# Cross-attention with two score spans: probabilities turned by VectorE in 32x32 blocks and carried across partitions by DMAs, main loop interleaved by feature tile

## The chip, the cores and the metric

The kernel runs on one core of a Trainium2 chip. The metric is the time of the whole program on the device in microseconds (us). A core has TensorE (matmuls), VectorE, ScalarE and GpSimd (element by element work), and SyncE, which here only issues DMAs; the engines run side by side and meet at semaphores. TensorE reads SBUF and writes PSUM, eight banks of 128 partitions x 512 fp32 values.

## The reference

`x` is 8 x 1024 x 640, the context 8 x 64 x 1024. The first 56 tokens are text, the last 8 are 4 dummy and 4 image tokens, whose scores get a mask. There are 20 heads of 32 features.

```python
q = _split_heads(hidden_states @ w_q, HEADS)
k = _split_heads(text @ w_k, HEADS)
v = _split_heads(text @ w_v, HEADS)
out_text = _merge_heads(_sdpa(q, k, v))
mask_ip = _ip_mask(bbox, B, S, hidden_states.dtype)
k_ip = _split_heads(ip_h @ w_k_ip, HEADS)
v_ip = _split_heads(ip_h @ w_v_ip, HEADS)
out_ip = _merge_heads(_sdpa(q, k_ip, v_ip, mask=mask_ip))
out = (out_text + IP_SCALE * out_ip) @ w_out + b_out + residual
```

`_sdpa` is softmax(q k / sqrt(32) + mask) v, one softmax over the text keys and another over the 8 image and dummy keys.

## The kernel before

Queries are worked on in 16 groups of 512 (two for each of the 8 batches). All is laid out with features first: `xT`, `qT` and the output have the feature in the partition, five tiles of 128 features (four heads each). For full precision every large product is made of parts: an operand is rounded to `hi` by ScalarE, `lo` is the rest (by VectorE or GpSimd), and `three` adds hi x hi, hi x lo and lo x hi (L97 to L99).

A setup of about 97 us makes keys and values of all batches, and the queries, scores and softmax of group 0. Then each group g is done in two stages on TensorE:

- `scores(g)`: 80 score matmuls (L203) in eight units of PSUM, the output product of group g-1 (`out_tile`, 75 matmuls of 512 columns), and the first two of the five query tiles of group g+1 (`q_steps`). Beside it ScalarE copies scores to `prob` (L209), GpSimd adds the mask and subtracts the maxima (L238, L169), VectorE finds maxima and sums (L224, L230), ScalarE takes exponentials (L216) and GpSimd multiplies by the inverse sums (L175). All this goes by tiles of 128 queries, `tile(t)`, 20 heads x 64 keys wide.
- `values(g)`: a pair p of heads (2 x 64 keys = 128 rows) needs its probabilities with the key in the partition. `transpose_tile` (L1189) turns four 128 x 128 squares of `prob` on TensorE into a PSUM bank, ScalarE rounds the bank to `pT_hi` (L695), VectorE subtracts to get `pT_lo` (L940). `pv_pair` multiplies both by the pair's values (L1204, L1205), ScalarE moves half of the result (L700), VectorE adds the halves to `o_raw` (L947), ScalarE and GpSimd split that into `oT_hi` (L704) and `oT_lo` (L533). Between pairs TensorE does the last three query tiles of group g+1.

VectorE also makes `xT_lo` (L111, both inputs in SBUF) and adds the residual to the output (L957); ScalarE makes the residual `res` (L710). SyncE loads `xin` (L466) and stores the output (L473). Each engine runs its own list in the order written; nothing is reordered.

## Time and profile before

| | us |
|---|---|
| median of three runs | 849.45 (849.35 to 849.67) |
| the profiled execution | 849.42 |
| its span, first to last instruction | 847.6 |
| busy TensorE | 840.3 (99%) |
| busy VectorE | 625.6 (74%) |
| busy ScalarE | 581.8 (69%) |
| busy GpSimd | 507.2 (60%) |

The busy time of an engine is what it worked within the span; TensorE's matmuls are pipelined, so its busy share tells that it is fed, not that each matmul runs at its peak. The granted TensorE clock is at its higher level (2.4 GHz) in every slice of the page. DMA engines are busy 22% of their time.

### The profile page before, as it was taken

How to read it: one execution, taken by the hardware profiler on the slowest of the kernel's cores; microseconds unless marked ns; L12 is line 12 of the kernel's file. 1: busy time of each engine (PE TensorE's matmuls, PEld its weight loads, DVE VectorE, ACT ScalarE, POOL GpSimd, SP SyncE). 2: the span in 40 equal slices, each digit the busy share in tenths (PEclk: the TensorE clock that was granted, in tenths of full speed). 3: DMA queues.
4: the chain of work that ended last, by engine and by line, in shares of the span. 5: the costliest groups of instructions: out<-in, count | busy, mean ns of one | idle time of the engine just before them, and what ended most of it. 6: DMA issues, size and time to landing. Idle time of an engine off the chain costs nothing.

```text
span 847.6 us, 13817 instructions
## 1 busy us (share of the span) xinstructions
PE 840.3 (99%) x5036; PEld 708.4 (84%) x5036; DVE 625.6 (74%) x923; ACT 581.8 (69%) x987; POOL 507.2 (60%) x405
## 2 busy tenths in 40 slices
PE   9999999999999999999999999999999999999998
PEld 8889888888888888888888888888888888888877
DVE  6839877695867768695867769586766869587785
ACT  7756676866767585776768586775768577674773
POOL 0059778293756749294755839385664929375581
PEclk9999999999999999999999999999999999999999
DMA  9934223012030402104030401204030310310012
GB/s 316 387 98 133 93 79 132 1 35 107 1 132 1 140 1 90 43 2 139 1 132 1 140 2 39 94 1 140 2 131 2 101 39 2 123 38 26 2 49 75
DMA packets 34295, 65.06 MB, mean 77 GB/s; under 512 B 4544, under 2 KB 6848, under 8 KB 34112
## 3 DMA queue, kind: packets, MB, share of 16 engines
q1 hardware_dynamic: 33952, 62.84, 21.6%
q10 hardware_dynamic: 288, 1.44, 0.4%
q8 instruction: 40, 0.66, 0.3%
q14 instruction: 15, 0.12, 0.0%
HBM read 40.34 MB, written 23.59 MB: 75 GB/s over the span
## 4 chain that ended last, share of the span: by engine, by line
PE 80%; POOL 14%; ACT 3%; issue 2%; DVE 0%; DMA 0%; ACTq 0%; SPq 0%; POOLq 0%; DVEq 0%
PE bank L97 18%; PE bank L99 18%; PE bank L98 18%; PE bank L1189 8%; POOL prob L169 7%; PE bank L203 6%; POOL prob L175 6%; PE bank L1204 4%; PE bank L1205 4%; ACT prob L209 2%; PE bank L1087 1%; PE bank L1095 1%; POOL wo_lo L498 1%; PE bank L1099 1%; POOL prob L238 1%
## 5 line engine op out<-in xcount | busy, mean ns | idle before, releaser
L533 POOL TENSOR_TENSOR oT_lo<-o_raw,oT_hi 128x512 fp32r<-128x512 f32 x63 | 81.4, 1293 | 208.1 <-ACT oT_hi L704 208.0
L947 DVE TENSOR_TENSOR o_raw<-bank,pv_part 64x512 f32<-64x512 f32 x160 | 110.2, 689 | 100.3 <-ACT pv_part L700 97.8
L169 POOL TENSOR_TENSOR prob<-prob,top 128x1120 f32<-128x1120 f32 x126 | 180.1, 1458 | 0.7 <-DVE top L224 0.7
L175 POOL TENSOR_TENSOR prob<-prob,inv 128x1120 f32<-128x1120 f32 x126 | 178.3, 1449 | 0.0
L97 PE MATMUL bank<-xT_hi,wq_hi 128*128 128x512 f32 x400 | 162.8, 407 | 0.0
L97 PE MATMUL bank<-oT_hi,wo_hi 128*128 128x512 f32 (+1 forms) x405 | 159.2, 393 | 2.0 <-ACT res L756 2.0
L98 PE MATMUL bank<-oT_lo,wo_hi 128*128 128x512 f32 (+1 forms) x405 | 156.7, 387 | 0.0
L99 PE MATMUL bank<-oT_hi,wo_lo 128*128 128x512 f32 (+1 forms) x405 | 156.7, 387 | 0.0
L99 PE MATMUL bank<-xT_hi,wq_lo 128*128 128x512 f32 x400 | 156.6, 391 | 0.0
L98 PE MATMUL bank<-xT_lo,wq_hi 128*128 128x512 f32 x400 | 155.9, 390 | 0.0
L940 DVE TENSOR_TENSOR pT_lo<-bank,pT_hi 128x512 fp32r<-128x512 f32 x158 | 102.0, 686 | 56.1 <-ACT pT_hi L695 54.1
L216 ACT ACTIVATE prob<-prob 128x1280 f32<-128x1280 f32 x64 | 81.7, 1277 | 78.2 <-POOL prob L169 78.2
L700 ACT ACTIVATE pv_part<-bank 64x512 f32<-64x512 f32 x160 | 94.8, 592 | 58.3 <-PE bank L1205 55.8
L224 DVE TENSOR_REDUCE top<-prob 128x20 f32<-128x1120 f32 (+1 forms) x128 | 98.2, 812 | 31.0 <-ACT prob L209 20.9
L125 ACT ACTIVATE qT<-bank 128x512 f32<-128x512 f32 x80 | 47.7, 596 | 86.6 <-PE bank L99 86.6
L230 DVE TENSOR_REDUCE total<-prob 128x20 f32<-128x1120 f32 (+1 forms) x128 | 97.9, 805 | 1.7 <-ACT prob L216 1.7
L97 PEld LDWEIGHTS bank<-oT_hi,wo_hi 128*128 128x128 f32 x405 | 76.1, 188 | 20.0 <-ACT res L756 2.4
L695 ACT ACTIVATE pT_hi<-bank 128x512 fp32r<-128x512 f32 x158 | 86.1, 596 | 8.0 <-PE bank L1189 6.4
L99 PEld LDWEIGHTS bank<-oT_hi,wo_lo 128*128 128x128 f32 x405 | 76.1, 188 | 15.7
L99 PEld LDWEIGHTS bank<-xT_hi,wq_lo 128*128 128x128 f32 x400 | 75.1, 188 | 16.4
L98 PEld LDWEIGHTS bank<-oT_lo,wo_hi 128*128 128x128 f32 x405 | 76.1, 188 | 14.7
L98 PEld LDWEIGHTS bank<-xT_lo,wq_hi 128*128 128x128 f32 x400 | 75.4, 189 | 13.3
(118 smaller groups left out, 1352.8 us busy)
## 6 DMA issues: line engine op xcount, KB each, us to landing
outT<-res SPq DMA_DIRECT2D x79, 256.0 KB, 6.7
xin<-in_xT SPq DMA_DIRECT2D x15, 1280.0 KB, 6.8
w_raw<-in_L_xattn_w_k SPq DMA_DIRECT2D x8, 320.0 KB, 5.4
w_raw<-in_L_xattn_w_k_ip SPq DMA_DIRECT2D x8, 320.0 KB, 5.7
w_raw<-in_L_xattn_w_v_ip SPq DMA_DIRECT2D x8, 320.0 KB, 4.3
w_raw<-in_L_xattn_w_v SPq DMA_DIRECT2D x8, 320.0 KB, 3.2
v_raw<-v_scratch SPq DMA_DIRECT2D x14, 140.0 KB
prob<-in_textT SPq DMA_DIRECT2D x8, 224.0 KB, 4.6
```

The lines of the kernel that those rows point to most:

```text
L97: nc.tensor.matmul(dst, a_hi, b_hi, start=first, stop=False)
L98: nc.tensor.matmul(dst, a_hi, b_lo, start=False, stop=False)
L99: return nc.tensor.matmul(dst, a_lo, b_hi, start=False, stop=last)
L169: ins = eng.tensor_tensor(s, s, top[:, t, n, :].unsqueeze(2).broadcast_to([P, HEADS, k1 - k0]), ALU.subtract)
L175: ins = eng.tensor_tensor(s, s, inv[:, t, n, :].unsqueeze(2).broadcast_to([P, HEADS, k1 - k0]), ALU.mult)
L216: nc.scalar.activation(prob[:, t * SW:(t + 1) * SW], prob[:, t * SW:(t + 1) * SW], ACT.Exp).then_inc(exp_done, 1)
L224: ins = nc.vector.tensor_reduce(top[:, t, n, :], tile(t)[:, :, k0:k1], AX.X, ALU.max)
L230: nc.vector.tensor_reduce(total[:, t, span, :], tile(t)[:, :, k0:k1], AX.X, ALU.add).then_inc(sum_done, 1)
L695: nc.scalar.activation(pT_pair(g, p)[0], pT_bank(g, p)[:], ACT.Copy).then_inc(pT_hi_done, 1)
L700: nc.scalar.activation(pv_part[own, :], v_bank[p % 2][other, :], ACT.Copy).then_inc(pv_moved, 1)
L940: nc.vector.tensor_tensor(lo, pT_bank(g, p)[:], hi.bitcast(F32), ALU.subtract).then_inc(pT_lo_done, 1)
L947: nc.vector.tensor_tensor(o_raw[own, m % 2, :], v_bank[p % 2][own, :], pv_part[own, :], ALU.add).then_inc(pv_added, 1)
```

## The change

The probabilities are no longer turned by TensorE. In place of four query tiles the softmax now goes by five chunks m, one for each feature tile: `chunk(m)` holds 4 heads x 4 tiles x 64 keys = 1024 columns. When a chunk is normalised, VectorE turns its 32x32 blocks in place of partition quarters (`turn`, one instruction for 1024 columns) into `stage`, and SyncE carries the blocks to the right quarter of the partitions, back into `prob` (`hand_over`: 16 DMAs of 32 partitions for each of three shares of a group: chunks 0 and 1, 2 and 3, 4). ScalarE rounds from there to `pT_hi`; `pT_lo` is made by VectorE for even pairs and by GpSimd for odd ones, both from SBUF. The columns of a pair come in another order, which `add_pv` undoes as it writes.

The main loop of TensorE is one list for each group g: pairs 0 and 1, scores of chunk 0 of g+1, output tiles 3 and 4 of g-1, the last step of its tiles 0 to 2, and then four times two pairs, one chunk of scores of g+1, three output steps of g and one query tile of g+2. The other engines' lists follow that. The residual is loaded from HBM (`load_res`) instead of copied by ScalarE, and the bias is added with it. `oT_lo` is all made by GpSimd. The special last group is gone, and so are the loops with a counter: each list is written out in full. `stage` has four slots; chunk 4 shares the slot of chunk 3.

```diff
+        def chunk(m):
+            return prob[:, m * CHUNK:(m + 1) * CHUNK].rearrange("p (r k) -> p r k", k=KEYS)
...
+            m, r = divmod(n, 2)
+            return prob[:, m * CHUNK:(m + 1) * CHUNK].rearrange("p (t r c) -> p r t c", r=2, c=PW)[:, r]
...
+        def turn(dve, g, m):
+
+            before = (g, 3) if m == 4 else (g - 1, 4) if m == 3 else (g - 1, m)
+            dve.wait_ge(prob_done, KD * g + m + 1)
+            if before[0] >= 0:
+                landed(dve, *before)
+            src = prob[:, m * CHUNK:(m + 1) * CHUNK].rearrange("p (t c i) -> p t c i", t=GT, i=QUAD)
+            dst = stage[:, stage_slot(m)].rearrange("p c (t i) -> p t c i", i=QUAD)
+            nc.vector.transpose(dst, src).then_inc(turned, 1)
...
+                def hand_over(g, share):
+                    m0, m1 = SHARES[share]
+                    turns = stage[:].rearrange("p s (h c) t -> p (s h) c t", c=QUADS)
+                    pairs = prob[:].rearrange("p (n q t) -> p n q t", q=QUADS, t=P)
+                    s0 = 2 * stage_slot(m0)
+                    sp.wait_ge(turned, KD * g + m1)
+                    for q in range(QUADS):
+                        for c in range(QUADS):
+                            sp.dma_start(pairs[c * QUAD:(c + 1) * QUAD, 2 * m0:2 * m1, q, :],
+                                         turns[q * QUAD:(q + 1) * QUAD, s0:s0 + 2 * (m1 - m0), c, :]).then_inc(pT_landed[share], 16)
...
+                    hand_over(g, 2)
+                    if g > 0:
+                        for m in OUT_ORDER:
+                            store(g - 1, m)
...
+                    if g + 1 < NG:
+                        hand_over(g + 1, 0)
+                    if g + 3 < NG:
+                        load_x(g + 3)
+                    load_res(g)
+                    if g + 1 < NG:
+                        hand_over(g + 1, 1)
...
+                    pool.wait_ge(pT_hi_done, PAIRS * g + p + 1)
+                    nc.gpsimd.tensor_tensor(pT_at(pT_lo, g, p), pT(p), pT_at(pT_hi, g, p).bitcast(F32), ALU.subtract).then_inc(pT_lo_pool, 1)
...
-                    act.wait_ge(pT_ready, PAIRS * g + p + 1)
-                    nc.scalar.activation(pT_pair(g, p)[0], pT_bank(g, p)[:], ACT.Copy).then_inc(pT_hi_done, 1)
+                    landed(act, g, p // 2)
+                    wait(act, pv_ready, PAIRS * g + p + 1 - P_RING)
+                    nc.scalar.activation(pT_at(pT_hi, g, p), pT(p), ACT.Copy).then_inc(pT_hi_done, 1)
...
+                    if more:
+                        pT_part(n, 0)
+                        pT_part(n, 1)
+                        pT_part(n, 2)
+                    if more_x:
+                        move_q(act, x, 3)
+                    if more:
+                        pT_part(n, 3)
...
+                    if more_x:
+                        x_lo_part(dve, x, 0)
                     add_pv(g, 0)
                     add_pv(g, 1)
-                    pT_part(g, 3)
-                    oT_part(g, 0)
+                    if more_x:
+                        x_lo_part(dve, x, 1)
+                        x_lo_part(dve, x, 2)
+                    if g > 0:
+                        output(g - 1, 3)
+                    if more_x:
+                        x_lo_part(dve, x, 3)
+                    if g > 0:
+                        sums(dve, g, 4)
+                        output(g - 1, 4)
+                        output(g - 1, 0)
+                    if more:
+                        maxima(dve, n, 0)
+                    if g > 0:
+                        output(g - 1, 1)
+                        output(g - 1, 2)
+                    if more_x:
+                        x_lo_part(dve, x, 4)
+
                     add_pv(g, 2)
                     pT_part(g, 4)
                     add_pv(g, 3)
-                    pT_part(g, 5)
-                    for p in range(4, PAIRS):
-                        add_pv(g, p)
-                        for n in last_transposes_of(p):
-                            pT_part(g, n)
-                    oT_part(g, KD - 1)
-
-                def values(g, build=False):
-                    pT_part(g, 0)
-                    pT_part(g, 1)
-                    if build:
-
-                        dve.wait_ge(v_stored, 48)
-                    for s in range(KD):
-                        for p in (2 * s, 2 * s + 1):
-                            add_pv(g, p)
-                        if s < KD - 1:
-                            for p in (2 * s + 2, 2 * s + 3):
-                                pT_part(g, p)
-
-                def group(g, u):
-                    softmax(g, u)
-                    values(g)
-
-                dve.wait_ge(v_zeroed, 1)
-                v_lo_part(dve, 0)
-                values(0, True)
-                softmax(1, 1)
-                values(1)
-                for b in range(1, B - 1):
-                    group(2 * b, 0)
-                    group(2 * b + 1, 1)
-                softmax(NG - 2, 0)
-                values(NG - 2)
-                last_softmax(NG - 1)
-                last_values(NG - 1)
-                for m in range(KD - 1):
-                    output(NG - 1, 1, m, last_banks)
-                for n, (bk, q) in enumerate(last_halves):
-                    dve.wait_ge(out_ready, KD * NG + n)
-                    r = res[:, 1, KD - 1, q]
-                    nc.vector.tensor_tensor(r, bk[:, 0:q.stop - q.start], r, ALU.add).then_inc(out_done, 1)
+                    turn(dve, g, 4)
+                    if more:
+                        maxima(dve, n, 1)
+                        sums(dve, n, 0)
+
+                    add_pv(g, 4)
+                    add_pv(g, 5)
+                    pT_part(g, 6)
+                    if more:
+                        sums(dve, n, 1)
+                        maxima(dve, n, 2)
+                        turn(dve, n, 0)
+                        turn(dve, n, 1)
+
+                    add_pv(g, 6)
+                    add_pv(g, 7)
+                    pT_part(g, 8)
+                    if more:
+                        maxima(dve, n, 3)
+                        sums(dve, n, 2)
+
+                    add_pv(g, 8)
+                    add_pv(g, 9)
+                    if more and n % GPB == 0:
+                        v_lo_part(dve, n // GPB)
+                    if more:
+                        sums(dve, n, 3)
+                        turn(dve, n, 2)
+                        maxima(dve, n, 4)
+                        pT_part(n, 0)
+                        pT_part(n, 2)
+                        turn(dve, n, 3)
...
-                def transpose_tile(g, p, t):
-                    src = prob[:, t * SW + p * P:t * SW + (p + 1) * P]
-                    return nc.tensor.transpose(pT_bank(g, p)[:, t * P:(t + 1) * P], src, ident[:])
...
+                for g in range(NG):
+                    pv_pair(g, 0)
+                    pv_pair(g, 1)
+                    if g + 1 < NG:
+                        next_scores(g + 1, 0)
+                    if g > 0:
+                        long_outs(g - 1)
+                        for m in range(3):
+                            out_step(g - 1, m, KD - 1)
...
+                        pv_pair(g, 2 * s)
+                        pv_pair(g, 2 * s + 1)
+                        if g + 1 < NG:
+                            next_scores(g + 1, s)
+                        wide_outs(g, s - 1)
+                        if g + 2 < NG:
+                            if s == 1:
+                                wait(pe, out_done, outs_before(g - 1, 3) + 1)
+                            pe.wait_ge(q_moved, KD * (g + 1) + KD - 1 if s == 1 else KD * (g + 2) + s - 1)
+                            q_steps(pe, g + 2, s - 1)
+                    if g + 2 < NG:
+                        pe.wait_ge(score_copied, UNITS * (g + 1) + 2 * KD - 1)
+                        q_steps(pe, g + 2, KD - 1)
+                wide_outs(NG - 1, KD - 1)
```

What stands in a row on TensorE between the pairs, before (in the stage of values; L1189 is the turning, L97 to L99 one step of a query tile):

```order
L1204 MATMUL bank<-pT_hi,v_parts 128x512
L1205 MATMUL bank<-pT_lo,v_parts 128x512
L1189 MATMUL bank<-ident,prob 128x128 x8
L97 MATMUL bank<-xT_hi,wq_hi 128x512
L98 MATMUL bank<-xT_lo,wq_hi 128x512
L99 MATMUL bank<-xT_hi,wq_lo 128x512
```

and now (L196 are the scores of one chunk, L100 to L102 one output step):

```order
L1166 MATMUL bank<-pT_hi,v_parts 128x512
L1167 MATMUL bank<-pT_lo,v_parts 128x512
L196 MATMUL bank<-k_diag,qT 128x128 x8
L100 MATMUL bank<-oT_hi,wo_hi 128x512
L101 MATMUL bank<-oT_lo,wo_hi 128x512
L102 MATMUL bank<-oT_hi,wo_lo 128x512
```

The turning is gone from between the pairs, and the scores, which stood in one block before the output product, have moved there in five pieces.

VectorE around the border of two groups, before (end of the softmax of a group, then its pairs):

```order
L957 TENSOR_TENSOR res<-bank,res 128x512
L230 TENSOR_REDUCE total<-prob 128x20 x2
L232 RECIPROCAL inv<-total 128x40
L940 TENSOR_TENSOR pT_lo<-bank,pT_hi 128x512 x2
L947 TENSOR_TENSOR o_raw<-bank,pv_part 64x512 x2
```

and now (L237 is `turn`, of chunk 2 and then of chunk 3; the next group begins at the first L117):

```order
L237 STREAM_TRANSPOSE stage<-prob 128x4x8x32
L216 TENSOR_REDUCE top<-prob 128x16 x2
L946 TENSOR_TENSOR pT_lo<-prob,pT_hi 128x512 x2
L237 STREAM_TRANSPOSE stage<-prob 128x4x8x32
L117 TENSOR_TENSOR xT_lo<-xin,xT_hi 128x512
L956 TENSOR_TENSOR o_raw<-bank,pv_part 64x4x4x32 x2
L117 TENSOR_TENSOR xT_lo<-xin,xT_hi 128x512 x2
L962 SCALAR_TENSOR_TENSOR res<-bank,bias,res 128x512
```

The turning of chunk 3 stands last in a group's list, behind two `pT_lo` of the next group, and all five `xT_lo` and five outputs stand at the head of the list, ahead of the second pair.

SyncE in one group, now (before there were one load and five stores, and in some groups the small ones of keys and values):

```order
L462 DMA prob<-stage 32x4x128 x16
L467 DMA xin<-in_xT 128x5x512
L471 DMA res<-in_xT 128x5x512
L462 DMA prob<-stage 32x4x128 x16
L462 DMA prob<-stage 32x2x128 x16
L497 DMA outT<-res 128x512 x5
```

These are `hand_over` of shares 0, 1 and 2 (L462), 48 DMAs for each group, with the two loads and the stores in the same list.

## Rows read from the trace of the kernel before

**Rows 1.** the page's first part: busy time of each engine over the span

```profile
PE 840.3 (99%) x5036; PEld 708.4 (84%) x5036; DVE 625.6 (74%) x923; ACT 581.8 (69%) x987; POOL 507.2 (60%) x405
```

**Rows 2.** busy us of each engine in five stretches of one group each (x is a count)

```profile
164.04:212.55 48.51, 48.46 (x291) 40.37 (x290) 36.40 (x53) 33.42 (x57) 30.37 (x24) 1.00 0.18 62
...
sum 241.50, PE 241.41 PEld 201.82 DVE 179.07 ACT 169.79 POOL 151.60; mean PE 48.28 PEld 40.36 DVE 35.81 ACT 33.96 POOL 30.32
```

**Rows 3.** TensorE by the chain of work that ended last, 305 to 320 us: start, us, what

```profile
305.38 0.88 PE bank L1189 x8
...
309.24 4.83 PE bank L203 x80
314.07 0.43 PE bank L97
314.50 0.23 PE bank L98
```

**Rows 4.** groups of instructions by line and shape: operands, shapes, count | busy us, mean ns | idle before

```profile
L947 DVE TENSOR_TENSOR o_raw<-bank,pv_part 64x512 f32<-64x512 f32 x160 | 110.2, 689 | 100.3 <-ACT pv_part L700 97.8
L940 DVE TENSOR_TENSOR pT_lo<-bank,pT_hi 128x512 fp32r<-128x512 f32 x158 | 102.0, 686 | 56.1 <-ACT pT_hi L695 54.1
...
L1189 PE MATMUL bank<-ident,prob 128*128 128x128 f32 x640 | 84.7, 273 | 0.3
L111 DVE TENSOR_TENSOR xT_lo<-xin,xT_hi 128x512 fp32r<-128x512 f32 x80 | 84.3, 1068 | 0.0
L224 DVE TENSOR_REDUCE top<-prob 128x20 f32<-128x1120 f32 x64 | 84.0, 1312 | 20.9 <-ACT prob L209 20.9
...
L533 POOL TENSOR_TENSOR oT_lo<-o_raw,oT_hi 128x512 fp32r<-128x512 f32 x63 | 81.4, 1293 | 208.1 <-ACT oT_hi L704 208.0
...
L704 ACT ACTIVATE oT_hi<-o_raw 128x512 fp32r<-128x512 f32 x80 | 51.0, 637 | 3.0 <-DVE o_raw L947 2.6
...
L175 DVE TENSOR_TENSOR prob<-prob,inv 128x1120 f32<-128x1120 f32 x1 | 2.4, 2417 | 0.0
```

**Rows 5.** one line's instructions, L111 and then L940: count, duration ns min/median/max

```profile
L111 DVE TENSOR_TENSOR xT_lo<-xin,xT_hi x80: 626/682/2551, 26.6 to 765.5; 128x512 fp32r<-128x512 f32 x80
L940 DVE TENSOR_TENSOR pT_lo<-bank,pT_hi x158: 673/686/693, 98.1 to 833.5; 128x512 fp32r<-128x512 f32 x158
```

**Rows 6.** VectorE in order of time: start us, us, line, operation, idle before

```profile
327.38 0.63 DVE L111 TENSOR_TENSOR xT_lo<-xin,xT_hi 128x512 fp32r<-128x512 f32 x1
...
330.43 2.51 DVE L111 TENSOR_TENSOR xT_lo<-xin,xT_hi 128x512 fp32r<-128x512 f32 x1
...
339.54 1.29 DVE L940 TENSOR_TENSOR pT_lo<-bank,pT_hi 128x512 fp32r<-128x512 f32 x2 [4.11 <-ACT pT_hi L695]
```

**Rows 7.** GpSimd in order of time, the same columns

```profile
327.29 10.88 POOL L175 TENSOR_TENSOR prob<-prob,inv 128x1120 f32<-128x1120 f32 x8
344.61 1.29 POOL L533 TENSOR_TENSOR oT_lo<-o_raw,oT_hi 128x512 fp32r<-128x512 f32 x1 [6.45 <-ACT oT_hi L704]
```

**Rows 8.** SyncE issuing DMAs, 3 to 5 us and later: start us, us, line, out<-in

```profile
3.06 0.43 SPq L413 DMA_DIRECT2D prob<-in_ipT  x1
3.53 0.43 SPq L407 DMA_DIRECT2D w_raw<-in_L_xattn_w_k_ip  x1
...
89.45 0.95 SPq L440 DMA_DIRECT2D v_raw<-v_text  x1
...
91.96 0.65 SPq L441 DMA_DIRECT2D v_raw<-v_ip  x1
...
235.92 2.74 SPq L473 DMA_DIRECT2D outT<-res  x5
```

**Rows 9.** the page's DMA issues: operands, queue, count, KB each, us to landing

```profile
xin<-in_xT SPq DMA_DIRECT2D x15, 1280.0 KB, 6.8
...
outT<-res SPq DMA_DIRECT2D x1, 128.0 KB, 1.8
```

**Rows 10.** the page's DMA queues: packets, MB, share of 16 engines

```profile
q1 hardware_dynamic: 33952, 62.84, 21.6%
```

More of the change, by code:

```diff
@@ L200, in score_units, with score_unit @@
+        def score_unit(pe, g, m):
+            pe.wait_ge(q_moved, KD * g + m + 1)
+            for t in range(GT):
                 q_cols = slice(t * P, (t + 1) * P)
@@ L575, in group @@
-                def group(g):
-                    softmax(g)
-                    values(g)
-                values(0, True)
-                group(1)
-                with pool.Fori(1, B - 1) as b:
-                    group(2 * b)
-                    group(2 * b + 1)
-                group(NG - 2)
-                last_softmax(NG - 1)
-                for m in range(KD):
-                    add_x(m)
-                for m in range(1, KD - 1):
-                    oT_part(NG - 1, m)
+                    nc.gpsimd.tensor_tensor(oT_at(oT_lo, g, m), o_raw[:, (KD * g + m) % 2, :], oT_at(oT_hi, g, m).bitcast(F32), ALU.subtract).then_inc(oT_lo_done, 1)
@@ L805, in group @@
-                def group(g, u, b):
-                    softmax(g, u, b)
-                    values(g)
                 v_hi_part(0)
@@ L898, in _ @@
                     lo_chunk(c)
-                for t in range(GT):
-                    maxima(dve, 0, t)
+                for m in range(KD):
+                    maxima(dve, 0, m)
                 lo_chunk(behind[0])
@@ L1022, in last_values @@
+                dve.wait_ge(v_zeroed, 1)
+                v_lo_part(dve, 0)
+                turn(dve, 0, 2)
+                turn(dve, 0, 3)
+                pT_part(0, 0)
+                pT_part(0, 2)
+                dve.wait_ge(v_stored, 48)
+                for g in range(NG):
+                    n, x = g + 1, g + 2
+                    more, more_x = n < NG, x < NG
+                    if more_x:
+                        x_lo_part(dve, x, 0)
                     add_pv(g, 0)
                     add_pv(g, 1)
-                    pT_part(g, 3)
@@ new lines, in _ @@
+                    add_pv(g, 8)
+                    add_pv(g, 9)
+                    if more and n % GPB == 0:
+                        v_lo_part(dve, n // GPB)
+                    if more:
+                        sums(dve, n, 3)
[4 more added lines that the diff above has]
+                        turn(dve, n, 3)
+                for m in OUT_ORDER:
+                    output(NG - 1, m)
@@ L1171, in _ @@
                         ins.then_inc(k_ipT_ready, 1)
[L1172 to L1173 removed]
+                for m in range(KD):
+                    if m == 0:
+                        pe.wait_ge(k_built, HPT)
+                    elif m >= 3:
+                        pe.wait_ge(score_copied, 2 * m - 4)
+                    score_unit(pe, 0, m)
                 for k in range(KC):
@@ new lines, in _, with pv_pair @@
+                pe.wait_ge(q_moved, KD + 2)
+                q_steps(pe, 1, 4)
+                pe.wait_ge(w_lo_done[0], len(dve_chunks))
+                def pv_pair(g, p):
+                    n = PAIRS * g + p
+                    if p == 0 and g % GPB == 0:
+                        pe.wait_ge(v_built, 2 * (g // GPB + 1))
+                    wait(pe, pv_added, n - 1)
+                    pe.wait_ge(pT_lo_pool if p % 2 else pT_lo_dve, KD * g + p // 2 + 1)
+                    v = v_parts[:, p, :, :].rearrange("p s c -> p (s c)")
+                    nc.tensor.matmul(v_bank[p % 2][:], v, pT_at(pT_hi, g, p), start=True, stop=False)
+                    nc.tensor.matmul(v_bank[p % 2][:], v, pT_at(pT_lo, g, p), start=False, stop=True).then_inc(pv_ready, 1)
@@ L1319, in group, with next_scores @@
[L1319 to L1330 removed]
+                def next_scores(g, m):
+                    if m == 0:
+                        pe.wait_ge(q_moved, KD * (g + 1))
+                        pe.wait_ge(score_copied, UNITS * g)
+                        if g % GPB == 0:
+                            pe.wait_ge(k_built, HPT * (g // GPB + 1))
+                    else:
+                        if m == 1 and g > 1:
+                            pe.wait_ge(out_done, outs_before(g - 2, 4) + 1)
+                        pe.wait_ge(score_copied, UNITS * g + 2 * m)
+                    score_unit(pe, g, m)
@@ new lines, in wide_outs, with long_outs @@
+                def wide_outs(g, k):
+                    for m in (3, 4, 0, 1, 2) if g == NG - 1 else range(3):
+                        if k == 0 and g > 0:
+                            pe.wait_ge(out_done, outs_before(g - 1, m) + 1)
+                        out_step(g, m, k)
+                def long_outs(g):
+                    pe.wait_ge(q_moved, KD * min(g + 3, NG) - (1 if g + 2 < NG else 0))
+                    for k in range(KD):
+                        out_step(g, 3, k)
+                    pe.wait_ge(score_copied, min(UNITS * (g + 2) + 1, UNITS * NG))
+                    for k in range(KD):
+                        out_step(g, 4, k)
```

776 lines of the change are left out of this document (288 added, 488 removed).

## The prediction

> **What bounds the kernel now.** I read the page's first part, then the busy time in single groups, then the chain that ended last, then the groups of instructions, and last the issue of DMAs. TensorE is busy 840.3 of the span's 847.6 us [rows 1]; a group takes 48.3 us on average and TensorE has no gap in it, while VectorE is busy 35.8, ScalarE 34.0 and GpSimd 30.3 us [rows 2]. So the period of a group is TensorE's own work, and what leaves TensorE's list leaves the time, until another engine's list is as long. In the chain the eight transposes between two pairs take 0.88 us, so 0.11 us each [rows 3]. 80 score matmuls take 4.83 us; the matmul of 512 columns behind them takes 0.43 in place of 0.23 us, so the step from scores to a full matmul costs 0.20 us [rows 3].
>
> **TensorE's part of the change.** It loses 640 transposes [rows 4], 640 x 0.11 = 70.4 us, or 4.4 us a group. The 170 matmuls of 512 columns of a group and its 80 score matmuls stay. The scores now stand in five places instead of one, so four more steps of 0.20 us in each of 15 groups: 60 x 0.20 = 12 us (between 0, if the step were hidden, and 12). TensorE's list for a group is then 48.3 - 4.4 + 0.8 = 44.7 us. Both ends of the program change: at the start query tiles 2 to 4 of group 1 no longer lie between pairs, at the end the hand-made last group is gone, and the last chunk is turned, carried, rounded, multiplied, added and split with only output steps beside it. I estimate 5 us for both (bounds 0 and 12: the carrying alone is some 9 us, of which output steps hide most). Against the profiled execution's 849.4 (span 847.6 and 1.8 around it; the median is 849.45, the same): 849.4 - 70.4 + 12 + 5 = **796 us** if TensorE never waits.
>
> **What the others get, for each group.** VectorE, from 35.8 us [rows 2]:
> - ten `pT_lo` from PSUM leave, 1.29 us for two [rows 6]: -6.5.
> - five `pT_lo` with both inputs in SBUF come. The same shape is `xT_lo`: 0.63 us when alone and 2.51 us when it starts while GpSimd is in a subtraction or multiplication [rows 5, 6, 7]; its mean is 1.07 [rows 4], about 1.0 from start to start. So +5.0, bounds 3.2 and 12.6.
> - five `turn` of 1024 columns come, an operation the trace doesn't have. The lower bound is a pass at the pace of the reduction (1312 ns for 1120 columns [rows 4]), 1.2 us; the upper is the pace of VectorE's slowest row, 2417 ns for 1120 [rows 4], 2.2 us. I take 1.2, since it has one input and one pass: +6.0, bounds 6.0 and 11.
> - one more chunk to reduce and invert +0.7, one `oT_lo` less -0.6 (estimates from the same rows).
>
> Sum 40.4 us, bounds 38.6 and 53. GpSimd: 30.3 + 1.3 for the fifth `oT_lo` + 5 x 1.29 = 6.5 for `pT_lo` [rows 4] + 1 for five smaller pieces instead of four + 1.6 of waiting for VectorE's two-input instructions (0 to 3.2) = 40.7 us. ScalarE loses the residual and stays near 31. So beside 44.7 us of TensorE stand 40.4 and 40.7: the cover falls from 12 and 18 us to 4.
>
> The Trainium skill, SBUF — State Buffer, "Who interferes with whom", says that a VectorE instruction with two SBUF inputs contends with a GpSimd instruction that reads SBUF, and that the second to issue waits for the whole of the first; `L940`, with PSUM as one input, never leaves 673 to 693 ns [rows 5], so the trace agrees. This speaks against the change, which moves five instructions from the free kind to the other and makes GpSimd busy nearly always. Vector Engine (DVE) Microarchitecture Reference, section 3.8, says that the 32x32 transpose sustains one element per cycle per lane; at its clock that would be 1.07 us for 1024, near my lower bound; no row here shows it.
>
> **The carrying.** 48 DMAs a group, all on SyncE. An issue costs 0.47 us from start to start at the program's start and 2.74/5 = 0.55 for stores, but 2.51/3 = 0.84 for the only three gaps between copies from SBUF to SBUF [rows 8]. I take 0.5, as those three also had few and odd partitions, 56 and 8. One share is 16 x 0.5 = 8 us and lands 2 us later (1.8 for the smallest [rows 9]). The data: 5 x 1024 columns x 128 partitions x 4 bytes = 2.6 MB, 5120 packets of 512 bytes a group, 320 for each DMA engine. At the mean time of a packet now (21.6% of 16 x 847.6 us over 33952 packets = 86 ns [rows 10]) that is 28 us, at its mean rate by bytes 8 us; the old traffic adds 11. So it fits in 44.7 us, and one share moves as fast as it is issued or 3 us slower.
>
> **Where it closes.** In steady state these form a ring through three lists: VectorE's `turn` of chunk 4 -> SyncE's share 2 (16 issues), five stores 2.7, now and then keys and values 1.2 -> share 0 of the next group (16 issues), landing 2 -> ScalarE's three `pT_hi` 1.9 [rows 4] -> VectorE's `pT_lo` 1.0 and `turn` of chunk 3 1.2 -> the head of VectorE's next list (five `xT_lo`, two additions, five outputs, sums of chunk 4, maxima of chunk 0: 5.0 + 1.4 + 3.4 + 1.9 + 1.3 = 13.0, durations by rows 4) -> an addition, `pT_lo`, an addition, `turn` of chunk 4 (3.6). Together 26.6 us + 32 issues. At 0.5 that is 42.6, under TensorE's 44.7; it reaches 44.7 at 0.57 and the present 48.3 at 0.68 us. The other place with little room is that head: TensorE asks for the third output bank 14.4 us into the group, and the 13.0 us of VectorE's head end at about 13.5. GpSimd can't begin a list before ScalarE's first `oT_hi`, some 8 us in, so its 40.7 us reach 4 us into the next group. Each delay there is one of TensorE's. I put 0.9 us of waiting on each of 15 groups, between 0 and 2: 13.5 us. **796 + 14 = 810 us**.
>
> **Rivals.**
> 1. *No waiting to speak of.* The slack of 4 us is enough; 796 to 800. For it: the ring at 0.47 is 41.6 us. Against it: three lists at over 90% of the period with fixed orders.
> 2. *VectorE and GpSimd become the bound through the shared port.* If the ten two-input instructions wait 1.6 us on average in place of 1.0 and GpSimd loses as much, VectorE is at 44 to 46 and with the waits of its ring a group takes some 47.3: 796 + 15 x 2.6 = 835 (822 to 848). For it: 2.51 [rows 6] and GpSimd's share going from 63% to 91%. Against: the mean of 80 `xT_lo`, most of which fell into GpSimd's busiest time, is 1.07.
> 3. *Slower: SyncE's issue sets the ring.* One mechanism, from 0.68 us an issue on. At 0.75 a group takes 26.6 + 24 = 50.6 and the time is 796 + 15 x 5.9 = 885; at 0.84 it is 925. For it: 0.84 for copies within SBUF [rows 8], and DMA engines at 86 ns a packet would take 8 x 86 = 0.69 for each issue and hold it back. Against it: every other row is at 0.43 to 0.55, whatever the number of pieces.
> 4. *Slower: `turn` takes two passes,* 2.2 us. VectorE is at 45.4 before it waits for anything, and the ring has two of them; a group takes 49 to 50: 796 + 15 x 4.7 = 866. For it only that VectorE's 4-byte transpose is in no row.
>
> That the change doesn't do what it says is no rival: no transpose stands between the pairs in the new list.
>
> **How the numbers follow.** Forecast, 801 to 821: 0.42. Rival 1: 0.13. Rival 2: 0.24. Rival 3: 0.13. Rival 4: 0.08. The predicted time is 810 us. Leaving out rivals 3 and 4 from 860 up is nearly 0.2, so the range goes from 796 to 855, which holds rivals 1 and 2 and the edge of 3 (0.69 us an issue gives 859). Within 0.2% of 849.4, about what a measurement of this kernel can tell from no change, is 0.03, taken from rivals 2 and 3; faster 0.77, slower 0.20.
>
> **What would show it.** No L1189 group, and full matmuls still 0.23 us apart: the 70 us. The first matmul behind each chunk of scores at 0.43: the 12 us. The `turn` group's mean at 1.2 or at 2.2 us: rivals 1 and 4 apart. `pT_lo` from SBUF at a mean of 1.0 or over 1.6, and GpSimd's waits: rival 2. Starts of the 48 issues 0.5 or over 0.68 us apart, and ScalarE waiting for the carried blocks: rival 3. Stretches from one group's scores to the next: 44.7 is rival 1, 45.6 the forecast, over 48.3 slower. The forecast is wrong at its root if TensorE's busy time doesn't fall by some 60 us, or if its waits are for something in none of the lists above.

## The result and the profile after

The changed kernel takes **875.5 us** (median of 4 runs, 873.9 to 879.7) beside 849.4 for the kernel before (849.35 to 849.67): ratio 1.030, 95% interval 1.028 to 1.033. It is slower by 26 us; forecast were 810 us and a range from 796 to 855. The profiled execution is the 873.9 one, with a span of 872.1 us.

The first part of its page, then the chain that ended last, by engine and by line (the lines that answer to [rows 1]):

```profile
span 872.1 us, 13091 instructions
...
PE 814.0 (93%) x4381; PEld 650.9 (75%) x4381; DVE 670.6 (77%) x983; ACT 541.3 (62%) x928; POOL 624.1 (72%) x576
...
PEclk9999989999999999899999999999999999999898
...
SPq 45%; DVE 17%; PE 15%; DMA 11%; issue 7%; ACT 4%; POOL 1%; ACTq 0%; DVEq 0%
```

TensorE lost only 26 us of busy time, where 58 were forecast, and now idles 58 us, where it idled 7. The chain runs through SyncE's queue for 45% of the span. The carrying DMAs are `L462`; its line (count, duration ns min/median/max) and the waits that name them:

```profile
L462 SPq DMA_DIRECT2D prob<-stage x768: 585/601/1712, 90.3 to 853.6; - x192
...
DMA to landing us min/median/max: 1.8/2.0/5.1
```
```profile
ACT pT_hi L720 <- DMA prob<-stage: 77.2, 31, 6.3
...
DVE pT_lo L946 <- ACT pT_hi L720: 55.3, 33, 6.3
...
PEld bank L1166 <- issue: 46.0, 31, 6.9
PE bank L1166 <- DVE pT_lo L946: 28.4, 11, 6.5
```

This is the forecast's ring, read backwards: TensorE's pairs (`L1166`) wait for `pT_lo`, it for `pT_hi`, and that for a landing. SyncE in order of time over one group, from the `turn` of chunk 4 at 368.01:

```profile
369.28 10.85 SPq L462 DMA_DIRECT2D prob<-stage  x16
380.18 2.65 SPq L497 DMA_DIRECT2D outT<-res  x5
382.87 11.21 SPq L462 DMA_DIRECT2D prob<-stage  x16
394.13 0.59 SPq L467 DMA_DIRECT2D xin<-in_xT  x1
394.77 0.54 SPq L471 DMA_DIRECT2D res<-in_xT  x1
399.79 0.59 SPq L462 DMA_DIRECT2D prob<-stage  x1
```

Share 2, five stores and share 0 of the next group stand without a gap: 10.9 + 2.7 + 11.2 us. Issues start 0.64 us apart, but 25 of the 768 take over 1 us, up to 1.71, so that a share costs 10.2 to 11.5 us, 0.64 to 0.72 us an issue (0.68 and 0.70 in the two above). What follows in the chain (start us, us, what) is a branch that the forecast's ring didn't have:

```profile
393.49 0.60 SPq L462
394.13 6.34 DMA xin<-in_xT
400.49 0.63 ACT xT_hi L113
...
414.96 1.25 DVE stage L237
```

Behind share 0 stands `load_x`, whose 6.34 us of landing are as long as the forecast's landing, `pT_hi`, `pT_lo` and `turn` together (6.1). 368.01 to 414.96 is a period of 46.95 us. The periods without key and value loads are 46.5 to 47.3 us, those with them 48.3 to 51.9; only the first and the last two are shorter, 44.9 to 45.4. From the first `turn` of chunk 4 to the last are 15 periods, the mean 47.62:

```profile
128.16 1.25 DVE L237 STREAM_TRANSPOSE stage<-prob 128x1024 f32<-128x1024 f32 x1
```
```profile
842.39 1.25 DVE L237 STREAM_TRANSPOSE stage<-prob 128x1024 f32<-128x1024 f32 x1
```

So the main loop is not slower than before. A group took 48.3 us there [rows 2] and takes 47.6 now, some 10 us less in 15 periods. What lies outside the periods took 847.6 - 15 x 48.3 = 123 us and takes 872.1 - 15 x 47.62 = 157.8, which is 35 us more. The ring explains why the forecast's gain is missing in the loop; that the kernel became slower comes from its two ends.

**TensorE's longer waits cost more than themselves.** Three stretches around the end of one of its waits (start:end, length, busy us of TensorE, its weight loads, VectorE, ScalarE and GpSimd, granted clock, DMA share, GB/s):

```profile
344.00:348.00 4.00, 0.62 (x3) 0.19 (x1) 0.69 (x1) 1.46 (x3) 0.23 (x1) 1.00 0.58 122
348.00:356.00 8.00, 7.51 (x29) 5.51 (x30) 6.12 (x7) 6.30 (x13) 6.44 (x5) 0.57 1.01 346
356.00:364.00 8.00, 8.00 (x37) 6.38 (x37) 6.32 (x10) 2.37 (x5) 4.39 (x5) 1.00 0.35 81
```

TensorE is idle for 3.4 us; in the 8 us behind it the granted clock is 0.57, mostly the lower of the two levels, full matmuls start 0.43 us apart and 16 scores take 2.0 us in place of 1.1; then it is at full again. That costs some 3 us more, and is why the lost time shows as busy time too. It is the largest case in the main loop: behind waits of 2.4, 2.6 and 2.2 us (to 250.9, 446.5 and 543.2 us) the granted clock is 0.79 over the next 8 us, and behind one of 1.8 us (to 639.0) it is 1.00.

The operations that were in doubt came out near the forecast (groups by line; busy us, mean ns, idle before):

```profile
L237 DVE STREAM_TRANSPOSE stage<-prob 128x1024 f32<-128x1024 f32 x80 | 97.2, 1224 | 1.4
...
L946 DVE TENSOR_TENSOR pT_lo<-prob,pT_hi 128x512 fp32r<-128x512 f32 x80 | 73.5, 919 | 56.3 <-ACT pT_hi L720 55.3
...
L117 DVE TENSOR_TENSOR xT_lo<-xin,xT_hi 128x512 fp32r<-128x512 f32 x80 | 64.6, 823 | 22.7 <-ACT xT_hi L113 22.1
```

### The profile page after: what moved, and what is told of

It reads as the page before. It is cut to its first block, busy times and chain, and to the rows that moved or that the text cites. A ratio compares the mean times of both kernels' runs of the same rounds, so it can differ in the third digit from the quotient of the medians.

```text
span 872.1 us, 13091 instructions
## 1 busy us (share of the span) xinstructions
PE 814.0 (93%) x4381; PEld 650.9 (75%) x4381; DVE 670.6 (77%) x983; ACT 541.3 (62%) x928; POOL 624.1 (72%) x576
## 3 DMA queue, kind: packets, MB, share of 16 engines
q1 hardware_dynamic: 138656, 125.93, 48.4%
## 4 chain that ended last, share of the span: by engine, by line
SPq 45%; DVE 17%; PE 15%; DMA 11%; issue 7%; ACT 4%; POOL 1%; ACTq 0%; DVEq 0%
SPq L462 39%; DMA xin<-in_xT 6%; DVE res L962 4%; SPq L497 4%; DVE xT_lo L117 3%; PE bank L100 3%; DVE stage L237 3%; PE bank L101 3%; PE bank L102 3%; DMA res<-in_xT 2%; DVE o_raw L956 2%; DMA prob<-stage 2%; PE bank L196 1%; ACT xT_hi L113 1%; DVE top L216 1%
## 5 line engine op out<-in xcount | busy, mean ns | idle before, releaser
L573 POOL TENSOR_TENSOR pT_lo<-prob,pT_hi 128x512 fp32r<-128x512 f32 x80 | 116.4, 1455 | 99.9 <-ACT pT_hi L720 99.6
L249 POOL TENSOR_TENSOR prob<-prob,top 128x896 f32<-128x896 f32 (+1 forms) x160 | 179.4, 1142 | 4.5 <-DVE top L216 4.1
L256 POOL TENSOR_TENSOR prob<-prob,inv 128x896 f32<-128x896 f32 (+1 forms) x160 | 172.6, 1101 | 11.3 <-DVE inv L224 10.6
L100 PE MATMUL bank<-oT_hi,wo_hi 128*128 128x512 f32 x400 | 168.9, 422 | 8.3 <-POOL oT_lo L569 4.7
L100 PE MATMUL bank<-xT_hi,wq_hi 128*128 128x512 f32 x400 | 156.0, 390 | 5.8 <-ACT qT L139 3.2
L101 PE MATMUL bank<-oT_lo,wo_hi 128*128 128x512 f32 x400 | 159.1, 398 | 0.0
L102 PE MATMUL bank<-oT_hi,wo_lo 128*128 128x512 f32 x400 | 158.6, 396 | 0.0
L102 PE MATMUL bank<-xT_hi,wq_lo 128*128 128x512 f32 x400 | 155.6, 389 | 0.0
L222 DVE TENSOR_REDUCE total<-prob 128x16 f32<-128x896 f32 (+1 forms) x160 | 101.7, 676 | 4.4 <-ACT prob L208 4.2
L100 PEld LDWEIGHTS bank<-oT_hi,wo_hi 128*128 128x128 f32 x400 | 76.8, 192 | 36.6 <-ACT prob L203 7.3
L1166 PE MATMUL bank<-pT_hi,v_parts 128*128 128x512 f32 x160 | 67.5, 422 | 38.9 <-DVE pT_lo L946 28.4
L196 PEld LDWEIGHTS bank<-k_diag,qT 64*128 64x128 f32 x1280 | 81.7, 196 | 28.7 <-issue 21.4
L216 DVE TENSOR_REDUCE top<-prob 128x16 f32<-128x896 f32 (+1 forms) x160 | 99.6, 664 | 2.1 <-POOL prob L243 1.3
L237 DVE STREAM_TRANSPOSE stage<-prob 128x1024 f32<-128x1024 f32 x80 | 97.2, 1224 | 1.4
L196 PE MATMUL bank<-k_diag,qT 64*128 64x128 f32 x1280 | 97.0, 294 | 0.1
L203 ACT ACTIVATE prob<-bank 128x512 f32<-128x512 f32 x160 | 85.5, 592 | 11.3 <-PE bank L196 11.1
```

Source lines behind the costliest of these rows:

```text
L100: nc.tensor.matmul(dst, a_hi, b_hi, start=first, stop=False)
L101: nc.tensor.matmul(dst, a_hi, b_lo, start=False, stop=False)
L102: return nc.tensor.matmul(dst, a_lo, b_hi, start=False, stop=last)
L196: ins = nc.tensor.matmul(s_bank(g, 2 * m + r)[:, t * PW:(t + 1) * PW], qT[rows, m, q_cols], k_diag[rows, m, :], start=True, stop=True)
L216: ins = nc.vector.tensor_reduce(top[:, m, n, :], chunk(m)[:, :, k0:k1], AX.X, ALU.max)
L237: nc.vector.transpose(dst, src).then_inc(turned, 1)
```

## Experiments

Theory A: SyncE's serial issue sets the period. Rivals: the shared port of VectorE and GpSimd (B), TensorE's own list or clock (C), the amount of data on the DMA engines (D). Edits are to the changed kernel. "Period" is the mean distance of the `turn`s of chunk 4.

| kernel | us | ratio to before, 95% interval |
|---|---|---|
| changed kernel | 875.5 | 1.030 (1.028 to 1.033) |
| e1 half the issues | 819.8 | 0.964 (0.962 to 0.966) |
| e2 half the pieces | 870.8 | 1.024 (1.023 to 1.026) |
| e3 share 2 from ScalarE | 875.2 | 1.029 (1.026 to 1.032) |
| e4 `load_x` first | 889.0 | 1.043 (1.039 to 1.047) |
| e5 both | 867.3 | 1.020 (1.019 to 1.022) |
| e6 over DRAM, `load_x` first | 829.2 | 0.975 (0.973 to 0.977) |
| e8 20 issues a share | 979.4 | 1.152 (1.150 to 1.153) |
| e9 `load_x(2)` early | 874.5 | 1.030 (1.028 to 1.031) |
| e10 e6 and e9 | 826.6 | 0.972 (0.971 to 0.974) |
| e11 over DRAM, `load_x` behind | 827.0 | 0.974 (0.972 to 0.976) |
| e12 e5, ScalarE's issues later | 926.5 | 1.090 (1.088 to 1.092) |
| e13 last group split over two engines | 883.2 | 1.039 (1.036 to 1.041) |
| e14 the same, on e11 and e9 | 838.2 | 0.984 (0.983 to 0.986) |
| e15 last group with half the issues | 870.8 | 1.026 (1.022 to 1.030) |
| e16 the same, on e11 | 824.3 | 0.969 (0.967 to 0.971) |

**Number of issues against amount of data: e1, e2, e8.**

```
e1:  for c in range(QUADS // 2):                 # 8 of 16 DMAs a share
e2:  pairs[..., 2 * m0:m0 + m1, q, :] <- turns[..., s0:s0 + m1 - m0, c, :]   # half of each
e8:  cuts = (0, m1 - m0, 2 * (m1 - m0)) if q == 0 else (0, 2 * (m1 - m0))    # 20, same data
```

> Only 8 of the 16 DMAs of each share are issued (those to the first 64 partitions); the other half of the turned probabilities is left out of the carrying, everything else is done. Theory A (SyncE's serial issue sets the ring, 0.70 us each with 32 of them in it): the ring falls from about 48 to about 26.6 + 16 x 0.70 = 37.8 us, TensorE's list of 44.7 to 45 us is the bound again, so 15 groups give back some 2.6 us each and the first share another 5: 815 to 835 us. Theory B (VectorE and GpSimd hold each other up) or C (TensorE's own list or clock is longer than I said): no change, 868 to 878. Theory D (the data on the DMA engines): the same as A, so the next kernel must tell A and D apart.

> All 48 DMAs of a group are issued, each with half of its pieces (half the bytes and half the packets); the other half is left out of the carrying. Theory A (number of issues): 870 to 877 us, no more than 5 below the changed kernel. Theory D (packets or bytes of the carried data fill the DMA engines and hold the issue back): as with half the issues, 815 to 835 us.

> Each share is carried by 20 DMAs in place of 16: the four from the first quadrant are cut into two with half of the pieces each. Bytes, packets and their size stay. Theory A: 8 more issues in the ring at 0.64 to 0.70 us each are 5.1 to 5.6 us a group, 15 to 16 groups: 77 to 90 us more, and with them a longer wait of TensorE and a lower granted clock behind each, so 950 to 975 us. If data or engines' work set the period: 875 to 885.

Halving the issues takes 56 us away, halving the data and keeping the issues 5, and four more issues a share with the same data add 104. So A stands, and B, C and D fall as what sets the period: e1 has VectorE's and GpSimd's work and TensorE's list unchanged, and e2 has the same half of the data as e1 and gains next to nothing. With e1 the period is TensorE's own: 45.13 us from 257.63 to 302.76, the starts of two `turn`s of chunk 4. e8 came out somewhat above its range. Its periods between 294.18 and 783.83 us are 54.41 on average, those of the changed kernel between 269.43 and 703.91 are 48.28: 6.1 us for 8 issues, 0.77 each. Of that 0.64 to 0.70 are the issues; the rest, longer waits with the lower clock behind them, I have only as an argument.

**What one issue costs: e7**, run once, 967.8 us with the added DMAs.

> The changed kernel with 128 more DMAs behind its last store, in eight runs of 16 from SyncE with nothing else going on, each run waited for: within SBUF 32 partitions x 4 pieces of 512 bytes (the form of the first two shares), x 2, x 1, 32 partitions x one piece of 2 KB, 8 partitions x 4 pieces, 128 partitions x one piece of 512 bytes, then 32 partitions x 4 pieces from SBUF to DRAM, and from DRAM to SBUF. If the cost of an issue is one of SyncE's own work for a transfer within SBUF, all six forms within SBUF are 0.60 to 0.65 us apart and those with DRAM at one end 0.45 to 0.55; if it is set by the number of pieces (packets that the engines must take in), the forms with fewer pieces fall to 0.3 to 0.5 us.

SyncE with nothing else going on; first four pieces of 512 bytes on 32 partitions, then one piece of 2 KB on 32, four pieces on 8 partitions, then SBUF to DRAM and DRAM to SBUF (the last two in one fence; each row is 16 issues):

```profile
876.79 10.25 SPq L548 DMA_DIRECT2D prob<-stage  x16
```
```profile
911.27 10.00 SPq L548 DMA_DIRECT2D prob<-stage  x16
```
```profile
922.72 11.73 SPq L548 DMA_DIRECT2D prob<-stage  x16
```
```profile
947.34 7.86 SPq L548 DMA_DIRECT2D to_dram<-stage  x16
956.56 7.42 SPq L548 DMA_DIRECT2D prob<-to_dram  x16
```

An issue within SBUF costs 0.64 us, with two pieces, one piece and 128 partitions as well (10.17, 10.05 and 10.20 for 16), and 0.73 on 8 partitions; with DRAM at one end it is 0.46 to 0.49. None of them takes over 0.77 us here; the long ones of 1.1 to 1.7 us stand only where the kernel's other work goes on. What in it makes them long, no run told.

The Trainium skill, Perfetto Trace Analysis, "What 'DMA-bound' means", names the issuing engine's sequencer as one of three ways to be bound by DMA, and says that large descriptors are what matters for it. The trace agrees with the first, by the chain above. With the second it doesn't: a piece of 2 KB in place of four of 512 bytes leaves an issue at 0.63 us, and only fewer issues help.

**The other branches: e3, e4, e5, e12.**

```
e3:  ScalarE issues share 2: 4 each behind oT_part(g, 1), move_pv(g, 4), move_pv(g, 5), oT_part(g, 2)
e4:  load_x(g + 3) ahead of hand_over(g + 1, 0)
e12: as e3 and e4, but 8 behind oT_part(g, 2) and 8 behind move_pv(g, 6)
```

> The 16 DMAs of the last share (chunk 4) are issued by ScalarE, four at each of four places between its pT_hi of pair 7 and its copy of pair 6, the rest by SyncE as before. Nothing is left out. Theory A: the ring no longer holds both shares (32 issues become 16 on SyncE), the period falls to TensorE's list or to ScalarE's (32.4 + 16 x 0.6 = 42 us busy): 820 to 845 us. Theories B and C: 868 to 885, since nothing but the queue of 16 issues changes and ScalarE gets 10 us more.

> load_x(g+3) is issued ahead of hand_over(g+1, 0) and no longer behind its 16 issues. Theory A with one ring alone: no change but 0.6 us more in the ring, 873 to 885 us. Theory A with a second branch of equal length (share 0, load_x, its landing of 6.3 us, xT_hi, VectorE's head), which the chain showed in every second group: that branch goes, the groups without key and value loads get shorter by 1 to 2 us, 860 to 872 us.

> Both edits together: the last share's 16 DMAs issued by ScalarE and load_x(g+3) ahead of hand_over(g+1, 0). Each alone gave nothing (875.2 and 889.0). Theory A2 (there are two rings of nearly equal length, one through both shares on SyncE, 26.6 + 32 issues, the other through share 0, then load_x, its landing of 6.3 us, xT_hi and VectorE's list up to the turn of chunk 1, about 28 + 11 + 7 = 46 to 48 us): with both opened the period falls to TensorE's list of 45 us, 815 to 840 us. Theory C (ScalarE with 16 more issues, or TensorE's own list and clock, is the limit behind the ring): 860 to 880.

> As the run with the last share from ScalarE and load_x first (867.3 us), but ScalarE's 16 issues stand eight and eight behind its oT_hi of tile 2 and its copy of pair 6, and no longer ahead of the exponentials of chunks 0 and 1. Theory A3 (there a third ring holds 32 issues of SyncE, those of shares 0 and 1, and about 12 of ScalarE: turns of chunks 0 and 1, share 0, turn of chunk 3, share 1, pT_hi of pairs 6 and 7, ScalarE's issues, exponentials, sums, the next turns): the ring loses some 8 us, the period falls towards TensorE's 45.1, and the time to 835 to 850 us; a rest stays, because pairs 8 and 9 land later. Rival: ScalarE's total work (32 + 10 us) sets the period, wherever its issues stand: 862 to 872.

None came out where theory A put it. e3 and e5 fell into the ranges of their rivals (868 to 885, 860 to 880), e4 and e12 outside of all. e3 takes 16 issues from SyncE and gains nothing: its chain goes from share 0 through `load_x`, a landing of 6.2 to 7.3 us and VectorE's head to the `turn` of chunk 4, and from there on through ScalarE, whose exponentials now wait behind its own issues (30 times, 55.9 us together), to the sums and the turns in front of the next share 0. e4 puts that load first and loses 13 us: the issue of the load, some 0.45 us, is then in the ring, and with its 1.3 MB under way share 0 takes 11.3 to 12.3 us, where it took 10.8 to 11.5 (both from 330 us on); the mean period goes from 47.6 to 48.7 us. With both (e5) the chain has a third ring, 47.7 us from 378.67 to 426.35: turns of chunks 0 and 1, share 0, `turn` of chunk 3, share 1, `pT_hi` of pairs 6 and 7, ScalarE's issues among its exponentials, sums, the next turns. e4's ring and e5's hold two shares of SyncE; e3's holds one and ScalarE's issues. e12 was to open the third and made all worse. ScalarE in order of time (`L752` are its issues):

```profile
443.22 4.50 ACTq L752 DMA_DIRECT2D prob<-stage  x7
447.77 0.59 ACT L724 ACTIVATE pv_part<-bank 64x512 f32<-64x512 f32 x1 [4.19 <-issue]
447.78 5.13 ACTq L752 DMA_DIRECT2D prob<-stage  x8
452.96 0.60 ACT L139 ACTIVATE qT<-bank 128x512 f32<-128x512 f32 x1 [4.60 <-issue]
```

Its copies out of PSUM wait behind blocks of eight issues (`qT` 14 times, 66.3 us together), TensorE waits 3.58 us for this `qT`, and its granted clock is 0.67 over the 8 us behind. An issue is work of the engine that issues: 16 of them fit into ScalarE's busy time by the sum (32 + 10 us), but not between two of its copies. Whether the third ring alone would have given 835 to 850 us stays open, as e12 put another wait in its place.

**Fewer issues by another route: e6, e11, e10, e9.**

```
for q in range(QUADS):                            # 4 DMAs of 32 partitions
    dma(p_scratch[share].rearrange("(c i) n q t -> q i n c t", c=QUADS)[q], turns[q * QUAD:(q + 1) * QUAD, s0:...])
# and once they have landed, one DMA of 128 partitions
dma(prob[:, m0 * CHUNK:m1 * CHUNK], p_scratch[share].rearrange("p n q t -> p (n q t)"))
```

> The carrying goes over DRAM: for each share four DMAs (one for each source quadrant, 32 partitions) write the turned blocks to a scratch tensor in the order of the destination, and one DMA of 128 partitions reads it back, so 15 issues a group on SyncE in place of 48; the bytes moved for the carrying double. load_x stands ahead of share 0. Theory A: a share costs 2.4 us of issue, some 3 of landing, 0.6 and some 4 of landing, about 10 us in place of 13, and SyncE is no longer serial through both shares, so the period is TensorE's 45 us: 805 to 835 us. If the amount of data on the DMA engines matters more than the issues: 860 us and above.

> The carrying over DRAM as in the run of 829.2 us, but with load_x(g+3) behind share 0 as in the changed kernel, so that only the route and the number of issues differ from the changed kernel. If the gain is that of 15 issues in place of 48: 826 to 834 us, since share 0 now takes some 10 us from its turn to its landing and the branch over load_x has slack again. If part of the gain came from the place of load_x: 840 us or more.

> The changed kernel with load_x(2) issued ahead of hand_over(0, 0), where the DMA that ScalarE waits for at the start of the main loop (chain: 10.2 us for xin from 106.8 us on) was behind 16 + 7 issues. The opening alone should get 6 to 11 us shorter: 864 to 870 us, if nothing else then holds the first group. If v_raw or the first shares are as late, it stays at 873 to 877.

> The carrying over DRAM (829.2 us) with load_x(2) issued ahead of hand_over(0, 0). TensorE is the bound in the main loop there (45.1 us a group), so a shorter opening should be seen whole: 819 to 824 us. If the opening is held by v_raw or the first share: 827 to 830.

15 issues a group in place of 48, with 170 MB moved in place of 128, give 829.2 and 827.0 us; both are faster than either kernel of this study. e11 differs from the changed kernel in the route alone. The place of `load_x`, worth 13 us in e4, doesn't matter here. e10's page and chain in mid-program (starts of two groups of scores, then of two `turn`s of chunk 4):

```profile
span 824.8 us, 12563 instructions
...
PE 799.8 (97%) x4381; PEld 649.8 (79%) x4381; DVE 685.9 (83%) x983; ACT 541.1 (66%) x928; POOL 629.1 (76%) x576
```
```profile
442.99 1.09 PE bank L198 x16
```
```profile
439.37 1.25 DVE L239 STREAM_TRANSPOSE stage<-prob 128x1024 f32<-128x1024 f32 x1
```
```profile
484.50 1.25 DVE L239 STREAM_TRANSPOSE stage<-prob 128x1024 f32<-128x1024 f32 x1
```

The period is 45.13 us and TensorE is busy in all 620 us between 130 and 750 us: its list is the bound again. e9 gains nothing measurable in the changed kernel and e10 at most 3 us: with `load_x(2)` out of the way, the opening's chain goes through share 0 and the landing of `v_raw` instead.

**The close: e13, e14, e15, e16.** TensorE over the last 74 us, before, changed, and in e10:

```profile
773.60:847.60 74.00, 69.05 (x406) 56.24 (x404) 50.26 (x76) 46.54 (x78) 33.53 (x29) 1.00 0.10 36
```
```profile
798.10:872.10 74.00, 51.51 (x217) 38.22 (x217) 44.67 (x62) 29.79 (x49) 41.27 (x38) 0.88 0.43 132
```
```profile
750.80:824.80 74.00, 56.05 (x249) 41.38 (x247) 48.87 (x69) 33.93 (x56) 45.38 (x41) 0.91 0.56 176
```

It was idle for 5 us there and is now for 22 and 18, and its clock is lower.

```
e13, e14: last group's shares: 8 DMAs from SyncE, 8 from ScalarE at the same time
e15, e16: last group's shares: 8 DMAs from SyncE, the other 8 left out
```

> The changed kernel in which only the last group's three shares are issued by two engines, eight DMAs from SyncE and eight from ScalarE at the same time; nothing is left out. It measures what lies outside the 15 periods of the main loop. Theory E (in the last group TensorE has no query tiles and no scores to do, so the carrying is bare there: three shares of 13 us one behind the other): each share is 5 us shorter, and the end gets 8 to 15 us shorter: 859 to 867 us. Rival F (the end is held by the list of VectorE or by the last output): 872 to 877.

> The carrying over DRAM with load_x behind share 0 (827.0 us), with load_x(2) ahead of hand_over(0, 0), and the last group carried directly, eight DMAs from SyncE and eight from ScalarE for each share (7 us in place of 11 to 13). Theory E: 812 to 820 us. Rival F: 824 to 828.

> The changed kernel in which the last group's three shares are issued by SyncE alone and only 8 DMAs each (the other half of the last group's carrying is left out); ScalarE's list is untouched, unlike in the kernel with the last group split over two engines (883.2 us). Theory E (the carrying is bare in the last group): three shares, each 8 issues of 0.64 to 0.70 us shorter, of which shares 0 and 1 partly lie beside the last full group: 10 to 16 us less, 859 to 866 us. Rival F (the close is held by the lists): 871 to 876.

> The carrying over DRAM with load_x behind share 0 (827.0 us), the last group's three shares carried directly by SyncE with only 8 DMAs each (half of the last group's carrying is left out). A share takes 5.1 + 2 = 7 us in place of 10 to 13. Theory E: 9 to 15 us less, 812 to 818 us. Rival F: 824 to 828. What is left above 803 (the forecast's list with the measured 45.1 us a group) is then the opening and the lower granted clock behind TensorE's waits.

e13 and e14 were to shorten the close and lengthened it by 8 and 11 us. ScalarE in e14 (`L239` are its issues of share 1):

```profile
789.07 5.44 ACTq L239 DMA_DIRECT2D prob<-stage  x8
794.56 1.21 ACT L750 ACTIVATE pv_part<-bank 64x512 f32<-64x512 f32 x2 [10.38 <-issue]
```

Of the 10.4 us that `pv_part` stood back, 5.4 are the issues; the rest is the wait of these issues for their `turn`, which ScalarE's list now holds too. e15 and e16, which touch no other list, gain about 5 us (the intervals of e15 and the changed kernel overlap) and 3 us (those of e16 and e11 touch): e16 in rival F's range, e15 at its edge. The last 74 us of the changed kernel's chain are for half issues of SyncE (`L462`, 50%), but 24 fewer of them, some 16 us, give back only these 5. So the bare carrying is a small part. The rest lies in the lists: in the last full group TensorE has no query tiles left, 75 x 0.23 = 17 us less to do, while VectorE and GpSimd have nearly their whole list, and the last period is still 43.7 us in e10 (754.36 to 798.01, TensorE busy in 33.7 of them at a granted clock of 0.88), not 28. That the lists do it is read from the traces; no run took them apart.

## Why the prediction was wrong

- **The step that failed: "I take 0.5, as those three also had few and odd partitions".** [rows 8] had one price for transfers within SBUF, 0.84 us, and all rows at 0.43 to 0.55 had DRAM at one end. The kind of the two ends decides (0.64 against 0.46 to 0.49 in e7). Few partitions add 0.09 there, which makes 0.73 and not 0.84; what the rest was stays open. So 0.84 was too high, but the value was to be taken between 0.55 and 0.84, not below both. In the running kernel long single issues bring it to 0.64 to 0.72.
- **The ring's form was right.** The 26.6 us hold 1.2 for key and value loads; without them and with the 22.1 us of the two shares shown above the sum is 47.5 us, and that group took 46.95. The mean of 47.62 would be 26.6 + 32 x 0.66. Rival 3, at 0.13, named the mechanism that set the period. Its result, a loop slower than before, didn't come: 0.68 us an issue would be 48.3. (Two of its numbers are wrong by its own formula: 0.69 gives 856 and not 859, 0.84 gives 928 and not 925.) The branch over `load_x`, its equal, was missing; its length shows as soon as the first is opened (e3).
- **The main loop's share of the miss.** 15 x (47.62 - 44.7) = 43.8 us over the 796 case, in place of the 14 taken for waits. The last of the 15 periods belongs to the close in part, as TensorE's own list is only some 28 us there, so the border to the next term isn't sharp.
- **"+5 for both ends" was the second term that failed.** 157.8 us lie outside the periods; the 796 case had 794.2 - 15 x 44.7 = 123.7. So the ends cost 34 us more than forecast. Most of that is there without the ring as well: in e10, with 15 periods from 123.93 to 798.01, it is 824.8 - 674.1 = 150.7. In the opening, 90 to 130 us, TensorE is busy 30.1 us where it was 40.0; in the close it idles 17 us more than before, and both have stretches at the lower clock. In the opening `load_x(2)` and `v_raw` stand behind the 16 issues of the first share. The forecast counted TensorE's instructions in the last groups and not the other lists, which don't shrink with them. Without the ring the time is 820 to 829 (e1, e6, e10): 10 to 19 above the forecast, and still inside its range. It took both terms to leave it.
- **What an idle TensorE costs afterwards had no term.** By the stretches above it was some 3 us behind the wait of 3.4 us and 1.6 behind each of the three of 2.2 to 2.6, together some 8 us of the main loop (estimates, from the granted clock and the busy time of 8 us), and more in the ends.
- **The transposes and the scores' step.** The list came out at 45.13 us, forecast 44.7. 16 scores take 1.09 us, 68 ns each, where 80 in a row took 60 ns each [rows 3]: a step costs 0.12 us at its start beside the 0.20 at its end. Full matmuls start 0.227 us apart (129.94 to 133.57 us in e10), so 170 x 0.227 + 5 x (1.09 + 0.20) = 45.0. With 48.3 - 4.4 for the transposes, 0.8 and 0.6 for the steps it is 45.3, so the 70 us fit what was measured.
- **Rivals 2 and 4 are out.** `turn` has 1224 ns (1.2 taken). `pT_lo` from SBUF has 919 ns and `xT_lo` 823, forecast 1.0; the slowest took 2.15 and 2.0 us. So some take three times the shortest (0.63 and 0.67), but the means stay low, and e1 and e10 run at TensorE's pace with all ten of these instructions. The pace of the Trainium skill for the transpose (Vector Engine (DVE) Microarchitecture Reference, section 3.8), by the prediction's estimate 1.07 us for 1024 columns, is 0.15 below the trace.
- **The data.** The DMA engines were busy 48.4% of the span, some 23 us a group, where the forecast had 28 and 11. That error was on the safe side, and the data set no period.

## To carry over

Before work is handed to DMAs, count issues, not bytes: multiply their number on the engine that issues by a price from a row with the same two ends (SBUF or DRAM), and put the product into each ring that passes through that engine's queue. Here a detour with a third of the issues beat the direct way though it moves twice the data. When the bounding engine's list gets shorter, work out the first and last two groups by all engines' lists as well, since there the others set the pace: here the loop became shorter and the program longer.

## What the runs showed of the hardware

- Issuing one DMA within SBUF costs SyncE 0.63 to 0.64 us whether it has 32 or 128 pieces, 32 or 128 partitions; on 8 partitions 0.73; to DRAM 0.49, from DRAM 0.46 (e7).
- In the changed kernel 25 of 768 such issues took over 1 us, up to 1.71, and alone (e7) none over 0.77; with 1.3 MB under way (e4) a share of 16 took 11.3 to 12.3 us instead of 10.8 to 11.5.
- Behind a wait of 3.4 us TensorE's granted clock was 0.57 over 8 us, behind waits of 2.2 to 2.6 us 0.79, behind one of 1.8 us 1.00.
- Eight issues on ScalarE take 5.1 to 5.6 us and hold its own next instruction up by 4.2 to 5.3 us (e12), and TensorE with it; where they also wait for their data, by up to 10.4 us (e14).
